# First layer's sums of squares: GpSimd adds the first tiles of a block, VectorE the last ones and both sums

## The reference, cut to what matters

```python
x_norm = xn / jnp.maximum(jnp.linalg.norm(xn, axis=-1, keepdims=True), 1e-12)   # over the 128 entries
mean_sim = jnp.einsum('nbl,mbl->nm', x_norm, x_norm) / B                         # over b (64) and l (128)
_, idx = jax.lax.top_k(mean_sim, k + 1)                                          # 153 of 512 are kept per row
...
out = jnp.einsum('sd,sbl->dbl', An, xw) + bias
```

## Time and profile before

| what | us |
|---|---|
| median of 3 runs | 1570.79 (1570.73 to 1571.62) |
| the profiled execution, its own time | 1571.14 |
| its span in the profile | 1569.3 |
| first stage, up to the first work of the next | 141.4 |
| TensorE busy in the whole span | 1460.9 (93%) |
| VectorE busy | 1191.6 (76%) |
| ScalarE busy | 884.5 (56%) |
| GpSimd busy | 541.4 (34%) |

### The profile page before, as it was taken

One profiled execution on the slowest core, in us unless ns is written; L12 is line 12 of the kernel. 1 busy time (PEld: TensorE's weight loads), 2 busy tenths in 40 slices (PEclk: granted clock), 3 DMA queues, 4 the chain that ended last, 5 costly groups with the idle time before them and its releaser, 6 DMA issues. The chain is left out here.

```text
span 1569.3 us, 27466 instructions
## 1 busy us (share of the span) xinstructions
PE 1460.9 (93%) x7672; PEld 1233.4 (79%) x7672; DVE 1191.6 (76%) x3055; ACT 884.5 (56%) x1579; POOL 541.4 (34%) x746
## 2 busy tenths in 40 slices
PE   6998996899999999999999999999998945999996
PEld 6887975688888888888888888877887944777774
DVE  5996997466667766677667776667776996999997
ACT  5754653346554565545655466554444942777775
POOL 5950010113331233312332123320200001999996
PEclk9999997899999999999999999999998976999998
DMA  9803953202121122211212112032431000444443
GB/s 363 282 1 134 395 188 108 68 21 81 67 80 43 51 80 67 80 40 54 80 67 80 40 54 79 29 139 91 154 109 34 0 0 21 128 147 141 141 146 107
DMA packets 81473, 156.59 MB, mean 100 GB/s; under 512 B 8781, under 2 KB 8909, under 8 KB 81421
## 3 DMA queue, kind: packets, MB, share of 16 engines
q1 hardware_dynamic: 81420, 155.95, 29.2%
HBM read 105.45 MB, written 50.46 MB: 99 GB/s over the span
## 5 line engine op out<-in xcount | busy, mean ns | idle before, releaser
L835 POOL TENSOR_TENSOR rs_a<-ve_a,neghalf 128x1 f32<-128x1 f32 x64 | 35.1, 548 | 398.5 <-DVE nm_a L829 398.5
L1107 PE MATMUL bank<-wov,ht_hi 128*128 128x512 f32 x512 | 161.5, 397 | 0.4 <-DVE y_lo L1498 0.4
L1498 DVE TENSOR_TENSOR y_lo<-bank,y_hi 128x512 fp32r<-128x512 f32 x128 | 84.3, 688 | 94.5 <-ACT y_hi L1246 94.3
L254 PE MATMUL bank<-xn_lo,xn_hi 128*128 128x512 f32 (+1 forms) x640 | 148.9, 363 | 3.9 <-DVE xn_lo L231 3.5
L226 ACT ACTIVATE xn_hi<-xn 128x512 fp32r<-128x512 f32 x128 | 80.8, 631 | 116.8 <-DVE xn L219 104.0
L1246 ACT ACTIVATE y_hi<-bank 128x512 fp32r<-128x512 f32 x128 | 72.4, 590 | 117.7 <-PE bank L1080 113.2
L1309 ACT ACTIVATE xo<-xo,nb_b,rs_b 128x512 f32<-128x512 f32 x64 | 52.2, 815 | 132.6 <-POOL nb_b L837 132.6
L1934 POOL TENSOR_TENSOR xw_lo<-xres,xw_hi 128x512 fp32r<-128x512 f32 x64 | 82.8, 1295 | 126.8 <-ACT xw_hi L1895 126.8
L245 PEld LDWEIGHTS bank<-xn_hi 128*128 128x128 f32 x512 | 96.4, 193 | 18.9 <-ACT xn_hi L226 1.7
L1080 PE MATMUL bank<-ht_hi,u_lang 128*128 128x512 f32 x320 | 109.9, 392 | 0.1
L1061 PE MATMUL bank<-an_hi,xw_hi 128*128 128x512 f32 x256 | 103.6, 405 | 6.4 <-DVE xw_lo L1498 3.2
(11 more groups left out here) (236 smaller groups left out, 4320.8 us busy)
## 6 DMA issues: line engine op xcount, KB each, us to landing
xw_dram<-stage SPq DMA_DIRECT2D x64, 256.0 KB, 5.3
stage<-xw_dram SPq DMA_DIRECT2D x64, 256.0 KB, 2.8
stage<-in_x SPq DMA_DIRECT2D x64, 256.0 KB, 2.7
between<-xo SPq DMA_DIRECT2D x64, 256.0 KB, 2.0
xres<-between SPq DMA_DIRECT2D x32, 512.0 KB, 3.7
xin<-between SPq DMA_DIRECT2D x64, 256.0 KB, 2.7
out<-xo SPq DMA_DIRECT2D x64, 256.0 KB, 2.0
xr<-in_x SPq DMA_DIRECT2D x16, 512.0 KB, 8.8
```

Source lines behind the costliest of these rows:

```text
L254: mm = self.nc.tensor.matmul(out, h[:, c * P:(c + 1) * P], l[:, a:b], start=(i == 0 and c != 1), stop=False, skip_group_check=True)
L1107: mm = nc.tensor.matmul(yp[i % 2][:], ht[a][:, c, i, :], wov[b][:, c, :], start=(c == 0 and n == 0), stop=(c == CH - 1 and n == 2))
L1498: nc.vector.tensor_tensor(lo, full, hi.bitcast(F32), ALU.subtract).then_inc(done, 1)
```

## The change

GpSimd keeps the first 5 of 8 tiles of blocks 2 to 6 (four additions each) and the first 10 of 16 of block 7 (nine additions), 29 in all. VectorE adds the others into a sum of its own (`acc_v`, one buffer, a slot that was free), two additions for a block of eight and five for block 7, and then adds `acc_v` to `acc` (`add_both`), 21 additions more than before. An addition of tile j stands in VectorE's step `square_at[j] + 2`, the joining one in step F-6, behind `normalise`, `low_part` and, where there is one, `invert`. TensorE's sums now wait for VectorE's joining addition. The first square of a block that VectorE adds waits there for the previous block's joining addition. The squares are made earlier too: 14 of them stand before ScalarE's loop, formerly 10, and each later one is about three steps earlier.

```diff
-    by_vector = 8
+    wide, acc_v = s.place("wide", SPARE + 2, (N,)), s.place("acc_v", SPARE + 3, (N,))
-    square_at = {j: -1 if j < 10 else int((j - 10) * 0.78) for j in range(nb)}
-    on_vector = lambda j: j < by_vector
+    square_at = {j: -1 if j < 14 else int((j - 14) * 0.78) for j in range(nb)}
+    own = {b.g: 0 if b.g < 2 else 5 * b.size // 8 for b in blocks}
+    on_vector = lambda j: j - block_of[j].first >= own[block_of[j].g]
+    def add_first(pool, j):
+        block = block_of[j]
+        total = acc[:, block.g % 2, :]
+        pool.wait_ge(squared, j + 1)
+        if j - block.first == 1:
+            pool.wait_ge(norms.n2_ok, block.g - 1)
+            norms.add(nc.gpsimd, total, tile_sq(j - 1), tile_sq(j), added_p)
+        else:
+            summed(pool, j - 1)
+            norms.add(nc.gpsimd, total, total, tile_sq(j), added_p)
+    def add_rest(dve, j):
+        block = block_of[j]
+        total = acc[:, block.g % 2, :] if block.g < 2 else acc_v[:]
+        dve.wait_ge(squared, j + 1)
+        if j - block.first == own[block.g] + 1:
+            if block.g >= 3:
+                dve.wait_ge(added_v, complete[block.g - 1])
+            norms.add(nc.vector, total, tile_sq(j - 1), tile_sq(j), added_v)
+        else:
+            summed(dve, j - 1)
+            norms.add(nc.vector, total, total, tile_sq(j), added_v)
+    def add_both(dve, block):
+        total = acc[:, block.g % 2, :]
+        dve.wait_ge(added_p, taken[block.first + own[block.g] - 1])
+        summed(dve, block.last - 1)
+        norms.add(nc.vector, total, total, acc_v[:], added_v)
     def gpsimd(pool):
         fill(pool)
-        for j in range(by_vector, nb):
-            if j > block_of[j].first:
-                add(pool, nc.gpsimd, j, added_p)
+        for j in range(nb):
+            if not on_vector(j) and j > block_of[j].first:
+                add_first(pool, j)
@@ vector, in the loop over i, behind normalise and low_part
             for block in blocks[1:]:
                 if block.invert_at == i:
                     norms.invert(dve, block)
+                if block.g >= 2:
+                    for j in range(block.first + own[block.g] + 1, block.last):
+                        if max(square_at[j] + 2, 0) == i:
+                            add_rest(dve, j)
+                    if block.sums_at == i:
+                        add_both(dve, block)
@@ tensor
         def block_sums(block):
-            summed(pe, block.last - 1)
+            pe.wait_ge(added_v, complete[block.g])
```

More of the change, by code:

```diff
@@ L276, with __init__ @@
 class Norms:
-    def __init__(self, nc, s, sb, sem, sq, acc, wide, banks, blocks):
-        self.nc, self.s, self.sq, self.acc, self.wide, self.banks, self.blocks = nc, s, sq, acc, wide, banks, blocks
+    def __init__(self, nc, s, sb, sem, acc, wide, banks, blocks):
+        self.nc, self.s, self.acc, self.wide, self.banks, self.blocks = nc, s, acc, wide, banks, blocks
         self.block_of = {j: block for block in blocks for j in range(block.first, block.last)}
@@ L285, in __init__, with add @@
             sem(n) for n in ("n2_ok", "n_capped", "n_inverted", "n_rooted"))
[L287 to L298, removed]
+    def add(self, vector, out, one, two, added):
+        return vector.tensor_tensor(out, one, two, ALU.add).then_inc(added, 1)
     def columns(self, block):
@@ L350, in first_similarity @@
     sq, acc = s.place("sq", EXTRA, (8, N)), s.place("acc", SPARE, (2, N))
-    wide = s.place("wide", SPARE + 2, (N,))
+    wide, acc_v = s.place("wide", SPARE + 2, (N,)), s.place("acc_v", SPARE + 3, (N,))
     def tiles(i, k):
@@ L359, in first_similarity @@
     sums = Sums(nc, s, sem, banks[:6], None)
-    norms = Norms(nc, s, sb, sem, lambda j: sq[:, j % 8, :], acc, wide[:], banks[6:8], blocks)
+    norms = Norms(nc, s, sb, sem, acc, wide[:], banks[6:8], blocks)
     block_of = norms.block_of
@@ L368, in first_similarity @@
     fill, shape = consts
-    square_at = {j: -1 if j < 10 else int((j - 10) * 0.78) for j in range(nb)}
-    on_vector = lambda j: j < by_vector
+    square_at = {j: -1 if j < 14 else int((j - 14) * 0.78) for j in range(nb)}
+    own = {b.g: 0 if b.g < 2 else 5 * b.size // 8 for b in blocks}
+    on_vector = lambda j: j - block_of[j].first >= own[block_of[j].g]
+    taken, complete, count_v, count_p = {}, {}, 0, 0
+    for block in blocks:
+        for j in range(block.first, block.last):
+            if on_vector(j):
+                count_v += j > block.first + own[block.g]
+                taken[j] = max(count_v, 1) if j > block.first + own[block.g] else count_v + 1
+            else:
+                count_p += j > block.first
+                taken[j] = count_p if j > block.first else count_p + 1
+        count_v += block.g >= 2
+        complete[block.g] = count_v
     def summed(eng, j):
[L373 to L376, removed]
+        eng.wait_ge(added_v if on_vector(j) else added_p, taken[j])
     def sync(sp):
@@ L414, in scalar @@
         exponentials(act)
-    def add(eng, vector, j, added):
+    tile_sq = lambda j: sq[:, j % 8, :]
+    def add_first(pool, j):
         block = block_of[j]
-        eng.wait_ge(squared, j + 1)
+        total = acc[:, block.g % 2, :]
+        pool.wait_ge(squared, j + 1)
         if j - block.first == 1:
-            if block.g >= 2:
-                eng.wait_ge(norms.n2_ok, block.g - 1)
-        else:
-            summed(eng, j - 1)
-        norms.add(vector, j, added)
+            pool.wait_ge(norms.n2_ok, block.g - 1)
+            norms.add(nc.gpsimd, total, tile_sq(j - 1), tile_sq(j), added_p)
+        else:
+            summed(pool, j - 1)
[16 more added lines that the diff above has]
+        norms.add(nc.vector, total, total, acc_v[:], added_v)
     def gpsimd(pool):
         fill(pool)
-        for j in range(by_vector, nb):
-            if j > block_of[j].first:
-                add(pool, nc.gpsimd, j, added_p)
+        for j in range(nb):
+            if not on_vector(j) and j > block_of[j].first:
+                add_first(pool, j)
     def vector(dve):
@@ L434, in vector @@
         for j in (1, 2, 3, 5):
-            add(dve, nc.vector, j, added_v)
+            add_rest(dve, j)
         norms.invert(dve, blocks[0])
         for j in (6, 7):
-            add(dve, nc.vector, j, added_v)
+            add_rest(dve, j)
         for i in range(nb):
```

## The result

The changed kernel takes 1573.99 us (median of 20 runs, 1572.89 to 1575.82), the one before in the same series 1570.85 us. The ratio is 1.0020, 95% interval 1.0013 to 1.0027: slower by 3.1 us or 0.2%. The forecast was "no change" with 1570.8. The measured time lies inside the stated range (1566.9 to 1574.2), but only 0.2 us from its upper end, and on the side and near the price of rival (a), 1573.5.

What follows compares the result with a forecast made beforehand. The prediction took the stage to be TensorE's, with VectorE nearly as full. Its terms summed to -0.1 - 0.9 + 1.0 + 0 = 0.0 us, so 1570.8 us by the median, range 1566.9 to 1574.2.

Steps and rivals of the forecast that it cites:

- rival (a): VectorE becomes the bound and TensorE waits for its remainders ahead of 80 us: +2.7 us, 1573.5 us; chance 0.20.
- the three places: TensorE's stops: 0.62 us at 26.31 and 0.71 at 41.58 for GpSimd additions, 3.51 ahead of crosses at 85.22 for VectorE.
- the stop of step 32: TensorE's 3.51 us stop ahead of the crosses at 85.22, behind VectorE's six small operations, with half clock following.
- The start: Four more squares delay the first matmul, but the wait at 26.31 goes: 0.1 us gained, between 0.2 gained and 0.5 lost.
- The wait at 41.58: TensorE's wait for block 3's last GpSimd addition goes, VectorE's joining one being ready earlier: 0.9 us gained, or 0.
- VectorE's load per block: Between two inversions, 2.0 us less blocking against 1.8 to 2.2 us of added VectorE additions: even on the mean.
- The cover of 0.7 us per block: Slack between VectorE's busy 13.69 us between two inversions and the 14.36 us TensorE needs per block.
- deciding point (0.6 us): VectorE time lost per GpSimd addition from which the slack is used up and TensorE waits for remainders; forecast took 0.5.
- Steps 20 to 28: Five VectorE additions fall together between two inversions: 1.0 us lost, bounds 0 and 2.0.
- Step 32, 0: GpSimd still has three additions left beside VectorE's six small operations, so stop and half clock stay: 0, bounds 2.9 gained, 0.4 lost.
- rival (b): GpSimd is further ahead at step 32, shorter stop, clock stays at 2.4 GHz: 3.9 us faster, 1566.9 us; chance 0.17.
- Step 33 to the end: Six VectorE additions between steps 37 and 42, but GpSimd idle from about 87 us; TensorE stays without a gap: 0.

Runs made afterwards that it cites:

- one addition and the joining one: Changed kernel with GpSimd taking 6 of 8 tiles (12 of 16) instead of 5 (10), VectorE 14 additional additions instead of 21: 1571.53 us, ratio 1.0002.

## Why the prediction was right or wrong, point by point

*What bounds the kernel.* Right as far as it went: the three places and nothing else. But I treated the stop of step 32 as pure loss. It also covered GpSimd's lateness in the last block, as the move of the small operations showed (a wait of 3.3 us in its place).

*The start, 0.1 gained.* The first rounding came at 15.7 and 16.3 and the first matmul at 16.4 and 17.0, not at 17.2. The sums of block 2 are at 25.23 and 25.78 against 26.31 and 25.73 of before: 0 to 1.1 gained. The term lies in that range, but two profiles of one kernel differ by as much as the term could be tested on.

*The wait at 41.58, 0.9 gained.* The wait for GpSimd went, and the schedule alone shows most of the gain (14.6 us from the sums of block 2 to those of 3 instead of 15.3, with all additions still GpSimd's). So the earlier squares are enough to remove it; I had put it down to the split. In the changed kernel this distance is 15.8 us in one profile, 0.6 lost, with a wait of 0.92 us for a remainder on the way, and 14.5 in the other, 0.8 gained.

*VectorE's load per block, "even".* This is the step that failed. The sum let each GpSimd addition cost 0.5 us of blocking, from remainders that stand between normalisations, so that fewer of them would give back 2.0, 2.0 and 1.5 us in the three stretches above, 5.5 in all, and it gave VectorE's own additions no blocking. What was given back is 11.8 - 9.6 = 2.2 us, and 2.9 by the second profile, while the eleven additions brought 11 x 0.60 = 6.6 us: an addition left to GpSimd now costs 0.56 to 0.64 us instead of 0.47. The long case, 1.1 us, was in the rows of before, as the maximum of 1706 ns of the earlier trace rows; the sum went by the median. The cover of 0.7 us per block was gone, and from block 3 to 4 TensorE lost 1.6 and 1.4 us in the two profiles, costed at 0. Rival (a) had this mechanism, and its deciding point (0.6 us) and its price in all (+2.7) were right. Its parts were not: 0.8 us in block 4 and 2.0 in block 5 were 1.6 and 0.7. It got a chance of 0.20 because I held that the waits for inversions would absorb it. They were used up: VectorE reached the inversion at 43.54 late. Its sign, TensorE waiting for L231 for more than 2 us before step 32, came true in the first profile (2.15 us) and not in the second (1.24).

*Steps 20 to 28, 1.0 us.* VectorE's distance between the inversions was 16.02 us where 15.55 was worked out, and TensorE fell back 0.7 us from the sums of block 4 to tile 32 (1.76 - 1.07). Right in kind and near in size.

*Step 32, 0.* Right: three long operations, 81.13 to 85.64, and a stop of 3.45 us (3.43 in the second profile) as before, with the low clock behind it. In the kernel with only the squares earlier the stop was 3.16 us and the clock stayed up: the half of rival (b) that can come true, and it came without the split.

*Step 33 to the end, 0.* Right: TensorE is 1.8 us behind at tile 32 and 1.7 at the stage's end.

*Sum.* By the profiled stages the change costs 1.3 to 1.7 us, forecast 0, and the stage ends at 143.1 and 143.3, not within 1 us of 141.4. The term that was mis-sized is the load per block, 0 for 1.4 to 1.6. The other 1.4 to 1.8 us of the measured 3.1 stand behind the stage and had no term.

*The range.* That the time lies inside it is in part luck. Its upper end adds 2.0 + 0.9 + 0.5 = 3.4, but the 0.9 at 41.58 is a gain that may fail to come, so it drops out and can't be added. The terms' own bounds give 0.5 at the start, 2.0 in block 5 and 0.4 at step 32, +2.9 or 1573.7, and the measured 1573.99 is above that. Only with rival (a)'s 0.8 in block 4 added would the end cover it.

## What to carry to other kernels

An instruction moved from GpSimd to VectorE doesn't only bring its own time: if it reads two operands from SBUF, it also becomes something that the rest of GpSimd's work can block, and here it was blocked longest right behind another one of its kind. The rest of GpSimd's work can also get dearer: with pauses in it, its additions began just ahead of a remainder more often. Before splitting a sum between the two, try to give the slow engine its data earlier; here one constant in the order of the squares removed the waits at which the split was aimed. And a stop may cover another engine's lateness, so look for what comes due next before counting it as gain.

## What the hardware showed that was not expected

GpSimd and VectorE take turns, and what VectorE loses to one GpSimd addition depends on when it begins: 0.5 us where additions follow without a pause and a normalisation stands between VectorE's operations with two SBUF inputs, 1.1 us where two of these stand together (1.77 us for the addition at 36.44) and up to 1.1 us where GpSimd begins out of idle just ahead of one (1.75 us for the remainder at 34.77); alone either takes 0.68.

TensorE's granted clock stayed at the 2.4 GHz level behind a stop of 3.16 us, in the one profile with only the squares earlier. It fell to 1.2 GHz at stops of 3.26 us (small operations moved), 3.43 (one addition and the joining one, and the changed kernel again), 3.45 (changed) and 3.51 and 3.53 us (before). From block 5 to 6 the first of these kernels needed 1.8 us less than the kernel before, 0.35 of it for the shorter stop; the rest goes with the clock. These few profiles don't show that the length of the stop decides.
